# Second group's gathers moved behind the flag, coarser sampling of the edge ids, both first groups masked by VectorE

## The reference

```
h    = relu(layernorm(x))                       # 6250 x 256
out1 = segment_sum(edge, dst); out2 = segment_max(edge, dst)   # 6250 x 96 each
out3 = out1 / max(count, 1)
y    = relu(concat[h, out1, out2, out3, u[0]] @ W1 + b1) @ W2 + b2   # hidden 1024
out  = x + y + h
```

## Time and profile before

| what | value |
|---|---|
| median of 3 runs | 550.93 us (550.51 to 552.75) |
| the profiled execution's own time | 551.13 us |
| its span from first to last instruction | 549.3 us |
| PE busy | 498.4 us, 91% |
| DVE busy | 437.6 us, 80% |
| ACT busy | 391.6 us, 71% |
| POOL busy | 247.6 us, 45% |

### The profile page before, as it was taken

The page is one execution under the profiler, slowest core; times in us unless marked ns, Lnnn a source line. Parts: engine busy times, 40 slices in busy tenths (PEclk is TensorE's granted clock), DMA queues, the critical chain, the costliest instruction groups (busy, mean ns, idle before and its releaser), DMA issues.

```text
span 549.3 us, 9292 instructions
## 1 busy us (share of the span) xinstructions
PE 498.4 (91%) x3182; PEld 454.8 (83%) x3182; DVE 437.6 (80%) x766; ACT 391.6 (71%) x1136; POOL 247.6 (45%) x260
## 2 busy tenths in 40 slices
PE   0494999989999999998999999999999999999991
PEld 0253998879999999987988888888888888889990
DVE  4828886999898999989899898988988987539420
ACT  1655788888787979977787787786967785574430
POOL 2343434456355574848457367174372560300211
PEclk9998899999999999998999999999999999999997
DMA  2972443354445363654644356255253340100100
GB/s 102 286 276 84 123 127 105 104 196 143 158 124 198 98 220 104 189 200 158 198 136 153 119 172 189 82 180 178 72 185 126 120 147 8 39 1 1 39 20 19
DMA packets 18838, 71.14 MB, mean 130 GB/s; under 512 B 4571, under 2 KB 5755, under 8 KB 18776
## 3 DMA queue, kind: packets, MB, share of 16 engines
q0 software_dynamic: 15408, 65.72, 36.8%
q1 hardware_dynamic: 3378, 4.79, 2.8%
HBM read 64.09 MB, written 6.85 MB: 129 GB/s over the span
## 4 chain that ended last, share of the span: by engine, by line
PE 75%; DVE 13%; ACT 3%; issue 3%; another core or an unknown queue 2%; DMA 2%; POOL 0%; DVEq 0%; POOLq 0%; ACTq 0%
PE l1ps L687 30%; PE l1ps L691 15%; PE yps L705 14%; PE yps L709 7%; PE l1ps L694 4%; PE tps L672 3%; DVE work L911 2%; DVE work L900 2%; DVE work L922 1%; PE tpr L675 1%; DMA work<-in_dst 1%; DVE hl L1000 1%; DMA xr<-dstp,rowi 1%; ACT work L495 1%
## 5 line engine op out<-in xcount | busy, mean ns | idle before, releaser
L362 POOL DMA_INDIRECT work<-in_edge_attr,idx x98 | 124.4, 1269 | 169.8 <-DVE work L922 97.1
L504 ACT ACTIVATE hff<-l1ps,b1e 128x512 f32<-128x512 f32 (+2 forms) x128 | 74.7, 584 | 101.4 <-PE l1ps L694 98.3
L687 PE MATMUL l1ps<-inh,w1h 128*128 128x512 f32 (+2 forms) x512 | 117.9, 352 | 5.2 <-issue 1.9
L495 ACT ACTIVATE work<-work,mk 128x96 f32<-128x96 f32 x411 | 116.0, 370 | 0.0
L691 PE MATMUL l1ps<-inl,w1h 128*128 128x512 f32 (+2 forms) x512 | 113.5, 344 | 0.9 <-DVE inl L1004 0.9
L687 PE MATMUL l1ps<-inh,w1l 128*128 128x512 f32 (+2 forms) x512 | 113.7, 344 | 0.0
L911 DVE TENSOR_TENSOR work<-work 128x192 f32<-128x192 f32 (+9 forms) x154 | 110.3, 738 | 1.1
L1000 DVE TENSOR_TENSOR hl<-hff,hh 128x512 fp32r<-128x512 f32 (+2 forms) x128 | 72.0, 567 | 47.3 <-ACT hh L506 32.7
L381 POOL DMA_INDIRECT out_y<-xr,oidx x49 | 68.1, 1391 | 88.7 <-DVE xr L1031 74.0
L705 PE MATMUL yps<-w2h,hh 128*128 128x256 f32 x392 | 99.6, 284 | 0.0
L705 PE MATMUL yps<-w2l,hh 128*128 128x256 f32 x392 | 98.2, 280 | 0.0
(11 more groups left out here) (162 smaller groups left out, 558.5 us busy)
## 6 DMA issues: line engine op xcount, KB each, us to landing
work<-in_L_gnn_W SPq DMA_DIRECT2D x2, 1024.0 KB, 6.2
work<-in_edge_attr,idx POOLq DMA_INDIRECT x98
xr<-in_L_gnn_W SPq DMA_DIRECT2D x1, 1024.0 KB
xr<-in_x,nid POOLq DMA_INDIRECT x49
out_y<-xr,oidx POOLq DMA_INDIRECT x49
work<-in_dst SPq DMA_DIRECT2D x1, 415.0 KB
dstp<-in_dst SPq DMA_DIRECT2D x1, 415.0 KB
hff<-in_L_gnn_W SPq DMA_DIRECT2D x3, 128.0 KB
```

The source lines that it names most:

```text
L362: pool.indirect_dma_start(out=runs[:, j * k * F:(j + 1) * k * F], out_offset=None, in_=edge, in_offset=bass.IndirectOffsetOnAxis(ap=idx[:, ...
L495: last = act.activation(es[g % 2][:, at * F:(at + 1) * F], run2(g)[:, at * F:(at + 1) * F], ACT.Copy, scale=mk[:, a + j, e:e + 1])
L504: act.activation(hf[C % 2][:, 0:cols], l1ps[C % 2][:, 0:cols], ACT.Relu, bias=b1e[:, m:m + 1])
L687: pe.matmul(ps, wt[:, c, ks(m)], inh[b % 2][:, c, 0:cols], start=(c == 0 and wt is w1h), stop=False)
```

## The change

It does six things. (1) Ids are sampled every 85 edges and not every 50: the compare has 125 x 1280 values, the sum 10 matmuls, a window 13 x 85 = 1105 ids. (2) On POOL, the first group's gathers all wait for `idx_ready` 3, and their order is run2, run1, both x tiles. (3) The second group's four gathers and batch 1's two x gathers stand behind the wait for the flag and the branch. (4) DVE masks all of group 1, inside `tree_head(1)`, as it does for group 0 in `tree_head(0)`; ACT's half is gone, and `own_path` with it. (5) In `tree_head` the mask comes ahead of the wait for run1. (6) `WARM` is 24 and not 20.

```diff
-    WARM = 20
+    WARM = 24
-    STEP = 50
+    STEP = 85
-    WIN = 21 * STEP
+    WIN = 13 * STEP
...
-            pool.wait_ge(idx_ready, 1)
-            gather_x(0, [0])
-            pool.wait_ge(idx_ready, 2)
-            gather_run1(0)
             pool.wait_ge(idx_ready, 3)
             gather_run2(0)
-            gather_x(0, list(range(1, width(0))))
-            pool.wait_ge(low_ps, W1A_LOWS)
-            gather_run2(1)
-            gather_run1(1)
-            gather_x(1, list(range(width(1))))
+            gather_run1(0)
+            gather_x(0, list(range(width(0))))
             pool.wait_ge(flag_ready, 1)
             general = pool.value_load(flag[0:1, 0:1], min_val=0, max_val=1)
...
             gather_general(0)
+            pool.wait_ge(low_ps, W1A_LOWS)
+            gather_run2(1)
+            gather_run1(1)
+            gather_x(1, list(range(width(1))))
...
             def mask(g, piece=0, pieces=1):
-                if g == 1:
-                    act.wait_ge(own_path, 1)
...
             low_parts(10, len(LOWS))
-            mask(1, 0, 2)
             norm(0, 0)
...
-            V.sem_inc(own_path, 1)
...
             def tree_head(g):
+                if g < 2:
+                    masks(g)
+                else:
+                    dve.wait_ge(masked, g - 1)
                 dve.wait_ge(run1_in[g % 2], run_count(g))
-                if g == 0:
-                    masks(0, 0, n)
-                else:
-                    dve.wait_ge(masked, g)
...
             V.tensor_tensor(out=b1e[:, :], in0=yps[0][:, 0:HC], in1=b1c[:, :], op=ALU.add).then_inc(bias_set, 1)
-            masks(1, 1, 1)
             in_low(0, 0)
             in_low(0, 1)
             tree_head(1)
```

More of the change, by code:

```diff
@@ L213, in gnn_block @@
     run1_in, run2_in = ([S(f"{n}{i}") for i in range(2)] for n in ("run1_in", "run2_in"))
-    masked, run2_used, tree_done, own_path = S("masked"), S("run2_used"), S("tree_done"), S("own_path")
+    masked, run2_used, tree_done = S("masked"), S("run2_used"), S("tree_done")
     stat_step, std_ready, ln_done = S("stat_step"), S("std_ready"), S("ln_done")
@@ L308, in _ @@
                 sp.wait_ge(bias_ps, 1)
-                sp.wait_ge(run1_in[1], run_count(1))
-                sp.wait_ge(run2_in[1], run_count(1))
                 for p, gout in enumerate((gsum, gmax)):
@@ L495, in mask @@
                     last = act.activation(es[g % 2][:, at * F:(at + 1) * F], run2(g)[:, at * F:(at + 1) * F], ACT.Copy, scale=mk[:, a + j, e:e + 1])
-                if piece == (0 if g == 1 else pieces - 1):
+                if piece == pieces - 1:
                     last.then_inc(masked, 1)
@@ L854, in _ @@
                 dve.wait_ge(bias_ps, 1)
-                dve.wait_ge(run1_in[1], run_count(1))
-                dve.wait_ge(run2_in[1], run_count(1))
                 V.memset(eT[F:F + 1, :], 1.0).then_inc(g_upd, 1)
@@ L872, in _, with masks @@
                 dve.wait_ge(g_out, 48)
-            V.sem_inc(own_path, 1)
             def slots(buf, n, per, lo, hi):
                 return buf[:, 0:n * per * F].rearrange("p (n e) -> p n e", n=n)[:, :, lo * F:hi * F]
-            def masks(g, j, w):
-                a, _, _, k2, _, _ = groups[g]
+            def masks(g):
+                a, n, _, k2, _, _ = groups[g]
                 dve.wait_ge(run2_in[g], run_count(g))
-                at = slice(j * k2 * F, (j + w) * k2 * F)
-                V.tensor_tensor(out=es[g][:, at].rearrange("p (n e f) -> p n e f", n=w, f=F), in0=run2(g)[:, at].rearrange("p (n e f) -> p n e f", n=w, f=F),
-                                in1=mk[:, a + j:a + j + w, 0:k2, None].broadcast_to([P, w, k2, F]), op=ALU.mult).then_inc(dve_step, 1)
+                V.tensor_tensor(out=es[g][:, 0:n * k2 * F].rearrange("p (n e f) -> p n e f", n=n, f=F), in0=run2(g).rearrange("p (n e f) -> p n e f", n=n, f=F),
+                                in1=mk[:, a:a + n, 0:k2, None].broadcast_to([P, n, k2, F]), op=ALU.mult).then_inc(dve_step, 1)
                 dve.wait_ge(dve_step, next(step))
```

## The result

The changed kernel takes **541.39 us** (median of 4 runs, 540.61 to 541.76) against 551.14 us for the kernel before on the same chip (4 runs, 550.51 to 552.75): a ratio of 0.9824, 95% interval 0.9801 to 0.9848. It is faster by 9.75 us. The profiled execution takes 541.06 us with a span of 539.3 us, against 551.13 and 549.3.

A forecast was written before the change was run, and what follows sets the result against it. Bound: a serial search with a 7.5 us wait, taken as the gathers' backlog, then PE's layers. -0.65 (ids) - 4.8 (wait) = -5.45 from 551.13 gives 545.7, or 545.5 us as median (0.2 lower); range 542.6 to 549.0.

The forecast's parts named there:

- What bounds the kernel: Start of the kernel: DVE waits 7.5 us for the sum of the checks, taken as delayed by a backlog of gathers.
- the wait's gain: DVE's wait for the flag's sum: moving six gathers, 1.93 MB at 400 GB/s, ends backlog and wait 4.8 us earlier.
- rival (b)'s first case: DVE's wait for the sum goes wholly: -6.95 us, 544.0 us; all of rival (b) had chance 0.15.
- The ids: Search at the start: sampling every 85 ids brings everything behind the window 0.65 us earlier, bounds -0.4 and -1.1.
- First group's order: POOL's first gathers, run2, run1, x: price 0, as weights cover it; without cover one gather, 1.25 us.
- Second group's landing: Six gathers behind the flag, issued from 35.5 to 43.0 us: they land in time for tree and batch 1, price 0.
- (c): Rival: a smaller delay returns at the second group's landing, 35 to 45 us: 2.6 us, 548.1 us, chance 0.12.
- (e): Rival: DVE's tree steps between flag and transposes come late, 0.7 us each, 11 us in all: 556.7 us, chance 0.05.
- The whole mask on DVE: Group 1's mask inside `tree_head(1)`: `lo(0)` 0.9 us later, covered by 2.9 us before PE needs it; price 0.
- Warm-up and clock: 24 warm-up matmuls before layer 1: 0 taken, bounds -2.3 (layer 1's first two steps at full clock) and +1.1 us.
- wait gone and clock high: Rival (b)'s double case, at the flag and layer 1: 541.7 us, outside the range; all of (b) had chance 0.15.

The follow-up runs named there:

- the small packets: Kernel before, with SP loading bias `b1` eight more times as 4-byte packets, 8192 in all: 552.29 us beside 551.81, ratio 1.0006 (chip D).
- the dose: Kernel before, with only the two gathers of the second group's run2 left ahead of the flag, the other four behind: 541.73 us (chip F), 541.17 us (chip C).
- the added gathers of chip C: Kernel before, with four more gathers of 393 KB ahead of the flag, the second group's masks waiting for them: 545.8 us, ratio 1.0083.
- the 543.35 beside the 552.39: Two runs on chip E of the kernel after with the second group's gathers put back ahead of the flag: 552.39 and 543.35 us.
- the gathers back: Kernel after, with the second group's gathers put back ahead of the wait for the flag: 541.43 us on chip F, ratio 0.9980.

## Why the prediction came out too high

**What bounds the kernel: right, on the chip it was read from.** A wait of 7.5 to 9.1 us for the sum is in the profiles of one kernel each on chips A, D and E; it is in no profile of chips B, C and F.

**The step that failed: the size of the wait's gain.** The prediction said that the backlog ends 4.8 us earlier by the gathers and 0.65 by the ids, and "with it DVE's wait". The first half held for the gathers: the traffic ended at about 33 us in place of some 37.6 (share 0.54 of 3 us in the earlier trace rows), 4.6 us earlier. The second half did not: the wait's end moved 6.22 us, down to where PE's own matmul ends, so nothing of the delay is left. The end of the wait fits POOL's issues better than the traffic. In the traces that have the wait, DVE reads the sum 3.39 us (35.42 to 38.81, the kernel before), 3.36 us (35.13 to 38.49, chip D) and 3.11 us (36.45 to 39.56, chip E) after POOL starts its last early gather. On chip D the small packets kept the engines occupied past that moment, and didn't hold the wait. In the kernel after, that gather starts at 29.20 instead of 35.42, 6.22 us earlier. By the same 3.1 to 3.4 us the sum would come at 32.3 to 32.6, and PE's matmul ends at about 32.57, so the two can't be told apart there: that the read moved by just the same 6.22 us is chance, as PE alone would have held it to that. With 1.25 us an issue from the earlier trace rows, six gathers were worth up to 7.5 us, less 1.3 for POOL's later start (22.93 for 21.65), and not 1.93 MB at 400 GB/s. That is rival (b)'s first case, which the prediction priced at 6.95. That the wait follows the last issue is a reading of three traces, and the dose that could have tested it met chips without the wait. ACT's stall before its piece `w1l` speaks against a plain tie: it ends 1.96 us (chip A, 37.38) and 1.91 us (chip D, 37.04) after POOL starts its last early gather, but on chip E 0.40 us before it (36.05). How a gather delays another engine's signal, no run shows, so the cause stays open.

**The ids.** -0.65 was forecast, about 0 came. POOL's wait for `dstp` ended at 8.8 as before, but the gather started at 9.67, 0.84 us behind it, where 0.3 had been assumed. It took 4.77 us instead of 4.24, where 0.1 more had been assumed. It landed at 14.44 against 14.23. PE's matmul of the flag didn't move either (32.43 for 32.29), so without this term the wait could give 6.3 at most, and gave 6.2.

**First group's order.** Price 0 was right as far as shown: in the kernel after the first mask starts at 35.20, behind the branch, and DVE doesn't wait for data there. ACT does, 1.0 us at 34.02 for the x tiles, which are now last; that wait isn't in the chain. The order alone was not tried.

**Second group's landing.** Right. POOL started at 34.80 (35.5 forecast) and finished its six at 44.7, later than the 43.0 forecast, because the four of edges took 1.30 to 1.60 us and the last of x 1.70 instead of 0.95. The head of the tree found them: no wait for them stands among the waits. Group 2's first gather, which was to be at most 0.8 us late, started at 45.03: with DVE 6.3 us earlier it was due at 41.5, so it was 3.6 us late behind the other six. It cost nothing either, as no DVE step up to 110 us waits for a gather. Rivals (c) and (e) didn't happen: no ownerless piece and no late tree step behind the flag. The Trainium skill, "DMA: Bandwidth & Descriptors", section Rules for kernel authors, says to issue early and wait late. Where the wait is absent the order is worth nothing either way (moved alone on chip B, 1.0003); on chip E the late order is 6.9 us better, so there the measurement goes against the rule.

**The whole mask on DVE.** Price 0 was right only with half clock as its cover. The kernel with the mask alone took 540.97 us. In the kernel after, layer 1 ran at full speed, and the cover was too short: ACT waits 1.0 us for `lo(0)` in this listing of waits, 47 to 60 us,

```profile
ACT hff L497 <- DVE hl L988: 1.0, 1, 1.0
```

and PE's layer 2 then comes in behind it. On chip C that wait was 2.1 us in two pieces.

**Warm-up and clock.** 0 was forecast, with -2.3 in the bounds. The bound is what came: layer 1 began at clock 1.00, and the distance grew by 2.35 us over its first two steps. But by the eighth step 1.35 us had been given back, the wait above among them. The reason that the prediction gave for the bound, that the first gap is closed, isn't what did it. On chips B, C and E the kernel before, or edits of it, go from the weight pieces into the warm-up without a gap too, and with 20 matmuls they then idle 2.2 to 2.4 us ahead of the transposes and start layer 1 at half clock; so does the kernel after with 20 (2.22 us). With 24 the idle is 1.75 us in the kernel after, and the clock is full. It is the second gap that counts, which the prediction expected to stay at 2 to 4 us: in all 20 traces of this case the clock at layer 1's start goes with its length, and it is full with 20 matmuls as well in the two where the idle is 2.00 us (`run2` ahead, chips F and C). The rule that gaps of idle make the clock fall, which the prediction took from the Trainium skill, "TensorE: Matmul & The Clock Gate", section HAM oscillation, agrees with these traces. In time, `WARM` alone did nothing that can be measured: 541.65 us in the kernel before with 24, 541.47 in the kernel after with 20. The 1.9 us behind 240 us had no step in the prediction. They are not the change's own: on chip C the kernel after has such a stretch too,

```profile
249.00:252.80 3.80, 3.80 (x16) 3.80 (x14) 3.73 (x6) 0.60 (x1) 2.33 (x2) 0.55 0.59 176
```

**The sum of the miss.** The span fell by 10.0 us, 4.55 more than the 5.45 forecast: 0.8 at the read of the sum (6.2 for the wait and the ids together), 0.5 from there to layer 1, 1.0 net in the first eight steps (2.35 less 1.35), 0.4 up to 240 us, 1.9 behind it. The case that occurred, wait gone and clock high, stood in the prediction at 541.7 and was left out of the range as a double. Each half had been worked out to within about 0.7 us; that both together were held to be too rare for the range is what put the time outside it. That 541.7 lies so near the measured 541.39 is in part luck: the ids' 0.65 didn't come, 1.35 us were given back in the first steps, and 1.9 us behind 240 us that nobody forecast made up for them.

## What to carry to other kernels

When a wait has no owner in the profile, date its end against each queue's last issue as well as against the traffic; here the bytes told a gain of 4.8 us and the issues one of 6.2 us, and the measured 6.2 us rules the bytes out. Before an experiment adds work ahead of a wait, its place in time should be checked in a trace of the chip that runs it: the added gathers of chip C came 5.6 us behind the wait that they were to lengthen. A gain that rests on a wait of unknown cause should be measured on several chips before it is believed: this change is worth 1.8% on one chip, and 0.2 and 0.1% on the two others where it ran whole. Work that is hidden behind a stretch at half clock has lost its cover as soon as the clock stays high.

## What the runs showed of the hardware

**Chips differ by 10 us on one program.** 133 runs of the kernel before on chips B, C and F, the ten sent as an experiment among them, lie between 538.5 and 546.1 us (but for one of 2778.52), 16 on A, D and E between 549.4 and 553.3; no run lies between. The traces tell the same two sets apart by something else: those from A, D and E hold 3698 to 3893 records of semaphore updates, those from B, C and F 5092 to 5165. That is so whether the trace has the wait or not, so missing records are no sign of the wait, as the expectation for the small packets had taken them to be. Traces that have the wait have other ownerless pieces too, as the 2.59 us of the earlier trace rows on chip A, 2.60 us at 205.37 and 2.74 at 234.61 on chip D. But the kernel after on chip A and the kernel with only the gathers moved on chip E have none between 60 and 250 us, though their gathers there are in the same order. So the lateness may belong to an execution as a whole, which six gathers in that place bring about on some chips; it would fit the 543.35 beside the 552.39 as well. That is open.

**On a chip without the wait times fall into groups that go with the mean granted clock.** Of the 12 runs with `WARM = 24`, five took 539.1 to 539.4 us at a clock of 0.990, five 541.6 to 541.9 at 0.986 to 0.987, one 543.7 at 0.978, one 544.1 at 0.984. Of the 25 runs of the kernel before on chip F, seven lie at 0.990 (538.8 to 540.2), twelve at 0.986 to 0.987, four at 0.978 (543.8 to 544.4) and two at 546 with 0.984. So a single execution of this kernel tells no difference below some 5 us. The clock also fell to 0.50 for some 3 us between 37 and 41 us, with PE busy, in the traces of 552.39 us (chip E), of the small packets (chip D) and of the gathers back on chip F, which has no wait; chip A's trace has 1.00 there. So it doesn't belong to the wait; why it fell, no run shows.
